# A gated delta rule in two chunks: cross products of the chunks' keys and queries in place of the state, and key products in half-precision pairs

## The chip, the cores and the metric

The kernel runs on one core of one Trainium2 chip. The metric is the device time of one execution in microseconds (us), the median of several runs. The weights and inputs are single precision in DRAM and so is the output.

## The reference, cut to what matters

One block of a network over x of 8 sequences, 256 tokens and 256 channels: adaptive layernorm, a gated delta rule with 16 key heads of 128 and two value heads of 128 for each, a gated output projection, then a feed-forward part that keeps 2 of 4 hidden values. The part that the change touches is this recurrence, for each sequence, head and value head:

```
q = l2norm(conv(x Wq)); k = l2norm(conv(x Wk)); v = conv(x Wv)
S = 0
for t in tokens:
    dv = beta_t * (v_t - k_t S)
    S  = decay_t * S + k_t dv^T
    o_t = q_t S
out = o * rsqrt(mean(o*o) + 1e-6) * norm_w * silu(z)
```

The kernel does not walk the tokens. It cuts a sequence into two chunks of 128 tokens. In a chunk, all dv come from one triangular system whose entries are products of keys with keys, times decays (the matrix A); outputs come from products of keys with queries, times decays (the matrix P). What the first chunk leaves for the second is the state S = K1^T (scaled values of chunk 1), 128 by 256; the second chunk needs K2 S and Q2 S.

## The kernel before, in words

The main part is a loop of 64 steps (16 heads by 4 blocks). A step is one head and one block of two sequences (BG = 2), that is four tiles of 128 tokens (TL = 4) and eight systems of 128 by 128 (U = 8). The steps are software pipelined by hand. Each engine has a function body(s0, s1, s2, s3) (lines 823, 1282, 1763 and 472), called 65 times, which writes out the order in which that engine does the work of four steps at once: s0 is new, s1 is one step older, s2 two, s3 three. Nothing else sets the order; each engine works through its list, and semaphores (sig, need) hold it where a result is missing. Two closing bodies (last_bodies, lines 996, 1354, 1834, 489) finish the last steps beside the beginning of the feed-forward part.

The chain of one step, with its names:

- project (line 597) multiplies hidden rows by the head's weights, both split into two half-precision parts, three products each: keys (0), queries (1), values (2, 3). last_tap (1084, ScalarE) and three convolve (1523, VectorE) for each make the convolution from PSUM into cc.
- turn_keys, turn_queries (633, 639) transpose cc; squares (1113) and squared_norms (1534), guarded_norms (1540), key_norm (382, GpSimd, a power of -0.5 into rn) and keys_normed (1120) give the normed keys kn; turn_normed (645) turns them back and keys_turned (1128) keeps them as knT, in single precision. queries_kept (1134) keeps the second chunk's queries as qT.
- key_key (651) and key_query (657) are four single-precision products each. decayed_keys (1565) and decayed_queries (1575) on VectorE multiply them with decays into at (ae) and pt.
- unit_system, first_inverse and six levels of level_rows, level_left, level_right (677 to 707, with 1160, 1164 and 1600) invert the systems by doubling, then residue (710) and refine (723) correct the inverse once. These all are half-precision products of 64 or 128 columns.
- first_values (733) solves for chunk 1; first_kept (1175) keeps the result twice: u0, and us scaled for the state. **state** (743) multiplies kn of chunk 1 with us, 256 columns, twice; **state_kept** (1187) copies it to st. key_state (757) multiplies knT of chunk 2 with st, query_state (763) qT with st. Then second_rest (1618), second_values (770), second_output (778, 1629), the norm and gate, and project_output (624).

Eight PSUM banks: bP (2) for project, decay_product, z_rows and outputs, bB (2) for the transposes and key products, bS (2) for residue to second_output, bL (2) for the levels. TensorE executes a single-precision product as two MATMUL records each with its own weight load; a transpose or a half-precision product is one.

The order at the head of TensorE's body, which the change rewrites:

```
if s0: bank_project(0, s0, s2); project(0, s0)
if s2: level_right(4, s2); level_left(4, s2)
if s1: key_query(s1)
if s2: level_rows(5, s2)
if s0: bank_project(1, s0, s2); project(1, s0)
```

Of the kernel before, what the change touches and what calls it, by code (L numbers as in the profile page):

```python
# [34 lines left out]
EPS_LN, EPS_RMS, EPS_K2 = 1e-5, 1e-6, 1e-24  # L35
GUARD = 0.25
# [9 lines left out]
def adaln_deltanet_ffn(nc, x, wh, nw, wba, dtb, alog, wgate, wup, wdown, cT, wmod, out):  # L46
    with ExitStack() as ctx:  # L47
# [56 lines left out]
        knT = sb("knT", [P, 2, TL, P])  # L104
        qT = sb("qT", [P, 2, BG, P])
# [16 lines left out]
        us, u0, st, rr, u1, qs = (sol[:, i] for i in range(6))  # L122
# [25 lines left out]
        small = knT[:].rearrange("p r t s -> p (r t s)")  # L148
# [14 lines left out]
        g_abs = qT[0:B].rearrange("p r g s -> p (r g s)").rearrange("p (h c) -> p h c", h=2)  # L163
# [59 lines left out]
        def all_steps(eng, body, last_bodies):  # L223
            for i in range(STEPS + 1):
                body(*lags(i))
            for i in range(STEPS + 1, STEPS + MOST):
                last_bodies(*lags(i)[2:])
# [23 lines left out]
        def _(sp):  # L251
# [38 lines left out]
            sp.wait_ge(sig("qk"), STEPS)  # L290
# [28 lines left out]
        def _(pool):  # L319
# [52 lines left out]
            def decay_operand(s):  # L372
# [4 lines left out]
                for part in range(2):  # L377
                    gp.tensor_tensor(g_le[:, part], le16[:].unsqueeze(1).broadcast_to([P, U, P]),  # L378
                                     hg[:, par(s), part, ts].rearrange("p t v -> p (t v)").unsqueeze(2)
                                     .broadcast_to([P, U, P]), ALU.mult).then_inc(sig("g_le"), 1)  # L380

# [90 lines left out]
            def body(s0, s1, s2, s3):  # L472
                if s3:
                    gate_output(s3)
                if s1:
                    first_inverse(s1)
                if s0:
                    decay_operand(s0)
                if s3:
                    output_scale(s3)  # L480
                    scaled_output(s3)
                if s1:
                    low_half(s1)
                if s0:
                    key_norm(s0)
                    masked_beta(s0)
                    decay_beta(s0)

            def last_bodies(s2, s3):

# [4 lines left out]
                else:  # L495
# [9 lines left out]
                else:  # L505
# [17 lines left out]
        def _(pe):  # L523
# [126 lines left out]

            def key_key(s):
                need(pe, "knT", N(s) + 1)
                for t in range(TL):
                    ins = m(bB[0][:, t * P:t * P + P], knT[:, ring(s), t], knT[:, ring(s), t])
                ins.then_inc(sig("kk_ps"), 1)

            def key_query(s):
                need(pe, "knT", N(s) + 1)
                for t in range(TL):
                    ins = m(bB[1][:, t * P:t * P + P], knT[:, ring(s), t], cc[:, 1, t * P:t * P + P])  # L660
                ins.then_inc(sig("kq_ps"), 1)

# [80 lines left out]
            def state(s):  # L743
                need(pe, "us", N(s) * 4 + 4)
                for g in range(BG):
                    ins = m(bS[1][:, g * C:g * C + C], kn[:, ring(s), 2 * g], us[:, g * C:g * C + C])
                ins.then_inc(sig("s_ps"), 1)

# [8 lines left out]
            def key_state(s):  # L757
                need(pe, "st", N(s) + 1)
                for g in range(BG):
                    ins = m(bS[1][:, g * C:g * C + C], knT[:, ring(s), 2 * g + 1], st[:, g * C:g * C + C])  # L760
                ins.then_inc(sig("ks_ps"), 1)

            def query_state(s):
                need(pe, "o0", N(s) + 1)
                need(pe, "qk", N(s) + 1)
                for g in range(BG):
                    ins = m(bS[0][:, g * C:g * C + C], qT[:, ring(s), g], st[:, g * C:g * C + C])
# [55 lines left out]
            def body(s0, s1, s2, s3):  # L823
# [3 lines left out]
                if s2:  # L827
                    level_right(4, s2)
                    level_left(4, s2)
                if s1:  # L830
                    key_query(s1)
                if s2:
                    level_rows(5, s2)
# [3 lines left out]
                if s2:  # L837
                    level_left(5, s2)
                if s1:
                    need(pe, "at", N(s1) + 1)  # L840
                    turn_values(0, s1)
                if s2:
                    level_right(5, s2)
                if s1:
                    need(pe, "pt", N(s1) + 1)
# [11 lines left out]
                if s0:  # L857
                    bank_project(3, s0, s2)
                    project(3, s0)
                if s2:  # L860
                    first_values(s2)
                if s1:
                    level_rows(0, s1)
                if s0:
                    need(pe, "iv", N(s0) * 2)
                    turn_keys(s0)
                    turn_queries(s0)
                if s3:
                    bank_turn_output(0, s0, s3)
                    turn_output(0, s3)  # L870
                if s2:
                    state(s2)
                if s1:
                    level_left(0, s1)
                if s2:
                    first_output(s2)
                if s1:
                    level_right(0, s1)
                if s2:
                    key_state(s2)  # L880
                if s3:
# [6 lines left out]
                if s0:  # L888
                    bank_decays(0, s0, s3)
                    decay_product(0, s0)  # L890
# [5 lines left out]
                if s0:  # L896
                    bank_decays(1, s0, s3)
                    decay_product(1, s0)
                    turn_normed(s0)
                if s2:  # L900
                    second_output(s2)
# [3 lines left out]
                if s1:  # L905
                    level_rows(2, s1)
                if s3:
                    bank_output(1, s0)
                    project_output(1, s3)
                if s1:  # L910
                    level_left(2, s1)
                    level_right(2, s1)
                if s0:
                    key_key(s0)
                if s1:
                    level_rows(3, s1)
                    bank_z(0, s0, s3)
                    z_rows(0, s1)
                    level_left(3, s1)
# [3 lines left out]
                    level_right(3, s1)  # L923
# [72 lines left out]
            def last_bodies(s2, s3):  # L996
                if s2:
                    level_right(4, s2)
                    level_left(4, s2)
                    level_rows(5, s2)  # L1000
                    level_left(5, s2)
# [4 lines left out]
                else:  # L1006
                    gate(1)
                bank_turn_output(0, None, s3)
                turn_output(0, s3)
                if s2:  # L1010
                    state(s2)
# [3 lines left out]
                    key_state(s2)  # L1015
                bank_turn_output(1, None, s3)
# [918 lines left out]
```

## Time and profile before

| | us |
|---|---|
| median of 3 runs | 2161.03 |
| lowest, highest | 2156.39, 2161.54 |
| the profiled execution's own time | 2155.69 |
| its span, first to last instruction | 2153.9 |
| mean granted TensorE clock | 0.986 of full speed |
| TensorE (PE) busy | 2068.8, 96% |
| VectorE (DVE) busy | 1890.6, 88% |
| ScalarE (ACT) busy | 1599.1, 74% |
| GpSimd (POOL) busy | 1317.9, 61% |

The profiled execution took 2155.69 us, 5.3 below the median of the runs; its span leaves out 1.8 us around it. Matmul ends are modelled and overlap the next matmul's start, so a block's cost on TensorE is read from its start to the start of the next block.

### The profile page before, as it was taken

The numbers are of one execution on the slowest core, as the hardware profiler recorded it, in microseconds if no ns is written. First come the engines' busy times: TensorE is split into PE (matmuls) and PEld (weight loads), VectorE is DVE, ScalarE is ACT, GpSimd is POOL, SyncE is SP. The second block draws the span as 40 slices with busy tenths as digits, with TensorE's granted clock in tenths as the row PEclk, the third lists the DMA queues.
The fourth block names the chain that finished last, engine by engine and source line by source line (L and its number), as shares of the span: only waits on it lengthen the run. The fifth ranks groups of instructions, "written<-read, shape, count | busy, mean of one in ns | idle before, by whom it ended". The sixth has DMA issues, their size and how long they took to land. (4 is left out here: it accounts for less than half of the span.)

```text
span 2153.9 us, 59276 instructions
## 1 busy us (share of the span) xinstructions
PE 2068.8 (96%) x22950; PEld 1709.5 (79%) x22950; DVE 1890.6 (88%) x3119; ACT 1599.1 (74%) x3275; POOL 1317.9 (61%) x832
## 2 busy tenths in 40 slices
PE   5599999999999999999999999999999999997898
PEld 4378888888888888888888888888888888886787
DVE  5689888899888898888898888898888998886898
ACT  3477788887778887878877878877888877776332
POOL 3456666666666666666666666666666666663452
PEclk7899999999999999999999999999999999999999
DMA  2000000000000000000000000000000000002000
GB/s 103 8 4 19 2 21 2 22 2 22 2 22 2 21 2 2 21 2 21 2 22 2 21 2 21 2 2 21 2 22 2 22 2 21 2 2 91 23 23 23
DMA packets 12392, 33.90 MB, mean 16 GB/s; under 512 B 1100, under 2 KB 9420, under 8 KB 9684
## 3 DMA queue, kind: packets, MB, share of 16 engines
q1 hardware_dynamic: 12116, 30.11, 4.0%
q8 instruction: 187, 3.06, 0.6%
q14 instruction: 89, 0.73, 0.1%
HBM read 27.99 MB, written 2.11 MB: 14 GB/s over the span
## 5 line engine op out<-in xcount | busy, mean ns | idle before, releaser
L1531 DVE SCALAR_TENSOR_TENSOR cc<-bank,wc,cc 128x510 f32<-128x510 f32 (+2 forms) x768 | 546.9, 739 | 20.7 <-ACT cc L1096 16.0
L527 PE MATMUL bank<-h,w 128*128 128x512 f16 (+1 forms) x1920 | 419.0, 359 | 9.6 <-DVE cc L1531 3.1
L1606 DVE TENSOR_TENSOR yl<-bank,mask 128x512 f16<-128x512 f32 x384 | 262.7, 684 | 63.9 <-PE bank L527 63.9
L527 PEld LDWEIGHTS bank<-h,w 128*128 128x128 f16 x1920 | 171.5, 98 | 149.6 <-DVE cc L1531 19.6
L1166 ACT ACTIVATE invT<-bank 128x512 f16<-128x512 f32 x384 | 235.6, 614 | 59.2 <-PE bank L527 59.2
L1162 ACT ACTIVATE inv<-bank 128x512 f16<-128x512 f32 x384 | 232.0, 604 | 59.4 <-PE bank L527 59.4
L1096 ACT ACTIVATE cc<-bank,wc 128x512 f32<-128x512 f32 x256 | 177.8, 695 | 129.1 <-PE bank L527 129.1
L378 POOL TENSOR_TENSOR g_le<-le,hg 128x1024 f16<-128x1024 f16 x128 | 239.7, 1893 | 23.4 <-DVE hc L1492 23.4
L404 POOL TENSOR_TENSOR e_b<-ae,b_le 128x1024 f32<-128x1024 f32 x64 | 151.5, 2367 | 158.7 <-ACT ae L1152 158.7
L446 POOL TENSOR_TENSOR invT<-maskT,a 128x1024 f16<-128x1024 f16 x64 | 136.0, 2126 | 161.6 <-DVE a L1589 161.6
L386 POOL TENSOR_TENSOR rn<-n2m,mhalf 128x4 f32<-128x4 f32 x64 | 64.8, 1013 | 276.2 <-DVE n2m L1546 276.2
L527 PE MATMUL bank<-inv,a 128*128 128x64 f16 (+1 forms) x3584 | 218.0, 197 | 3.2 <-ACT inv L1162 2.2
L527 PEld LDWEIGHTS bank<-inv,a 128*128 128x128 f16 x3584 | 188.9, 98 | 17.9 <-ACT inv L1162 2.9
L412 POOL TENSOR_TENSOR osq<-o,zg 128x1024 f32<-128x1024 f32 x64 | 151.4, 2366 | 75.3 <-DVE oss L1643 75.3
L527 PE MATMUL bank<-w,goT 128*128 128x256 f16 x1536 | 188.3, 273 | 2.1 <-DVE goT L1656 2.1
L527 PE MATMUL bank<-w,h 128*128 128x256 f16 x1536 | 189.3, 273 | 0.0
L527 PEld LDWEIGHTS bank<-yl,invT 128*128 128x128 f16 x3072 | 132.8, 98 | 52.0 <-DVE yl L1606 39.4
L527 PE MATMUL bank<-yl,invT 128*128 128x64 f16 x3072 | 153.8, 193 | 10.1 <-DVE yl L1606 10.1
L527 PEld LDWEIGHTS bank<-w,goT 128*128 128x128 f16 x1536 | 146.0, 98 | 17.7 <-DVE goT L1656 2.3
L1228 ACT ACTIVATE zth<-bank 128x512 f32<-128x512 f32 x128 | 76.1, 594 | 108.0 <-PE bank L527 108.0
L527 PE MATMUL bank<-invT,yl 128*128 128x64 f16 x3072 | 153.9, 193 | 1.9 <-DVE yl L1606 1.1
L527 PEld LDWEIGHTS bank<-w,h 128*128 128x128 f16 x1536 | 141.8, 98 | 14.9
(212 smaller groups left out, 5297.1 us busy)
## 6 DMA issues: line engine op xcount, KB each, us to landing
w_raw<-in_wh SPq DMA_DIRECT2D x16, 1032.0 KB, 4.8
v<-in_x SPq DMA_DIRECT2D x4, 512.0 KB, 3.8
out<-sol SPq DMA_DIRECT2D x16, 128.0 KB, 1.7
w_raw<-in_wgate SPq DMA_DIRECT2D x1, 1024.0 KB, 4.7
cc<-in_wup SPq DMA_DIRECT2D x1, 1024.0 KB, 4.7
pt<-gate_store SPq DMA_DIRECT2D x2, 512.0 KB, 4.3
ae<-in_wdown SPq DMA_DIRECT2D x1, 1024.0 KB, 6.7
sol<-gate_store SPq DMA_DIRECT2D x2, 512.0 KB, 5.8
```

The source lines that it names most:

```text
L378: gp.tensor_tensor(g_le[:, part], le16[:].unsqueeze(1).broadcast_to([P, U, P]), hg[:, par(s), part, ts].rearrange("p t v -> p (t v)").unsq ...
L386: gp.tensor_tensor(rn[:], n2m[:, blk(s), 0], mhalf[:, 0:TL], ALU.pow).then_inc(sig("rn"), 1)
L404: gp.tensor_tensor(e_b[:, :, 1:P + 1], e_raw, b_le[:], ALU.mult).then_inc(sig("eb"), 1)
L412: gp.tensor_tensor(flat(osq[:]), o[:].rearrange("p t v d -> p (t v d)"), flat(zg[:]), ALU.mult).then_inc(sig("zo"), 1)
L446: gp.tensor_tensor(invT[:, ring(s)], maskT1[:].unsqueeze(1).broadcast_to([P, U, P]), a1[:, ring(s)], ALU.mult).then_inc(sig("it"), 1)
L527: return mm(o_, l_, r_, start=start, stop=stop, skip_group_check=True)
L1096: A(cc[:, i], bP[i % 2][:], ACT.Copy, scale=wc[:, par(s), i, 3:4]).then_inc(sig("tap"), 1)
L1162: A(lefts(inv[:, ring(s)], l), halves(bL[0], l), ACT.Copy).then_inc(sig("x_ready"), 1)
L1166: A(rights(invT[:, ring(s)], l), halves(bL[1], l), ACT.Copy).then_inc(sig("xt_ready"), 1)
L1228: A(zth[:, 2 * h:2 * h + 2].rearrange("p t d -> p (t d)"), bP[h][:], ACT.Tanh, scale=0.5 / W_SCALE).then_inc(sig("z_tanh"), 1)
L1531: V.scalar_tensor_tensor(dst, src, wc[:, par(s), i, 3 - j:4 - j], dst, ALU.mult, ALU.add).then_inc(sig(f"conv{i}"), 1)
L1606: V.tensor_tensor(lefts(yl[:, l], l), halves(bL[0], l), left(mask[:, l + 1, :], l).unsqueeze(1).broadcast_to([P, U, HP // n_, n_]), ALU.mu ...
```

## The change

The state is gone. By K2 S = (K2 K1^T)(scaled values), the kernel multiplies chunk 1's keys with chunk 2's keys and with chunk 2's queries (key_cross, new), keeps both products (kx) and multiplies those with us. To have such products cheaply, normed keys and queries, scaled by 16, are kept as pairs of half-precision numbers (k16, q16, high and low part); key_key, key_query and key_cross are each three half-precision products in place of one of single precision. state, state_kept and queries_kept are gone, keys_low (VectorE), queries_high (ScalarE), queries_low (GpSimd) and cross_kept (ScalarE) are new, keys_turned writes the high part. The scale is taken out again in the decay columns in the setup. The bodies of all four engines are in a new order.

Products and copies:

```
-            def key_key(s):   m(bB[0][t], knT[t], knT[t])             (x4, f32)
-            def key_query(s): m(bB[1][t], knT[t], cc[1, t])           (x4, f32)
-            def state(s):     m(bS[1][g], kn[2g], us[g])              (x2, f32, 256 columns)
+            def key_pairs(o_, s, t, other, t_other):
+                for i, (a, b_) in enumerate(((0, 0), (0, 1), (1, 0))):
+                    ins = m(o_, k16[:, a, t], other[:, b_, t_other], start=(i == 0), stop=(i == 2))
+            def key_key(s):   need kh, kl; key_pairs(bB[0][t], s, t, k16, t)     (x4)
+            def key_query(s): need kl, ql; key_pairs(bB[1][t], s, t, q16, t)     (x4)
+            def key_cross(s):
+                need(pe, "pt", N(s) + 1)
+                for g in range(BG):
+                    for i, other in enumerate((k16, q16)):
+                        c_ = (g * 2 + i) * P
+                        ins = key_pairs(bB[1][:, c_:c_ + P], s, 2 * g, other, 2 * g + 1)
             def key_state(s):
-                need(pe, "st", N(s) + 1)
+                need(pe, "us", N(s) * 4 + 4)
+                need(pe, "kx", N(s) + 1)
-                    ins = m(bS[1][g], knT[:, ring(s), 2 * g + 1], st[g])
+                    ins = m(bS[1][g], kx[:, ring(s), g, 0], us[g])
             def query_state(s):
-                    ins = m(bS[0][g], qT[:, ring(s), g], st[g])
+                    ins = m(bS[0][g], kx[:, ring(s), g, 1], us[g])
```

The other engines:

```
 ScalarE
-                A(knT[:, ring(s)], grid(bB[1]), ACT.Copy).then_inc(sig("knT"), 1)
+                A(k16[:, 0], grid(bB[1]), ACT.Copy).then_inc(sig("kh"), 1)
-            def queries_kept(s): A(qT, second chunk of cc[:, 1], ACT.Copy)
+            def queries_high(s): A(q16[:, 0], cc[:, 1], ACT.Copy).then_inc(sig("qh"), 1)
+            def cross_kept(s):   need kx_ps; A(kx[:, ring(s)], grid(bB[1]), ACT.Copy).then_inc(sig("kx"), 1)
-            def state_kept(s):   A(st, bS[1][:], ACT.Copy).then_inc(sig("st"), 1)
 GpSimd
+            def queries_low(s):  need qh; gp.tensor_tensor(q16[:, 1], cc[:, 1], q16[:, 0], ALU.subtract)
 VectorE
+            def keys_low(s):     need kh; V.tensor_tensor(k16[:, 1], grid(bB[1]), k16[:, 0], ALU.subtract)
-  one tensor_scalar for the taps of a head
+  three tensor_scalar for the taps of a head (the queries' tap times 16)
+  setup: one tensor_scalar more over cols[:, BETA]
```

TensorE's body, new order in full, in place of lines 823 to 923:

```
project(0,s0) key_query(s1) level_left(4,s2) project(1,s0) level_rows(5,s2) level_right(4,s2)
key_cross(s1) turn_values(0,s1) level_left(5,s2) level_right(5,s2) turn_values(1,s1) residue(s2)
project(2,s0) turn_system(s1) refine(s2) project(3,s0) level_rows(0,s1) first_values(s2)
turn_keys(s0) level_right(0,s1) turn_queries(s0) level_left(0,s1) key_state(s2) first_output(s2)
turn_output(0,s3) turn_output(1,s3) query_state(s2) level_rows(1,s1) second_values(s2)
level_left(1,s1) level_right(1,s1) decay_product(0,s0) second_output(s2) level_rows(2,s1)
decay_product(1,s0) turn_normed(s0) project_output(0,s3) project_output(1,s3) level_left(2,s1)
key_key(s0) level_right(2,s1) level_rows(3,s1) z_rows(0,s1) level_right(3,s1) level_left(3,s1)
z_rows(1,s1) level_rows(4,s1)
```

On VectorE decayed_queries moves from behind level_rows(5) of the next body to the end of its own body, as decayed_queries(s0), so that it stands ahead of the next body's first convolve; keys_low(s0) stands between level_rows(2) and output_sums. On ScalarE cross_kept(s1) stands behind inverse_right(4), queries_high(s0) behind inverse_right(2), and high_half moves from the next body to a place between inverse_left(3) and inverse_right(3). On GpSimd the order becomes gate_output, queries_low, low_half, output_scale, first_inverse, decay_operand, masked_beta, scaled_output, key_norm, decay_beta. turn_values(1) now waits for kx in place of pt.

## Rows read from the trace of the kernel before

**Rows 1.** The page, busy time of each engine, its share, and instructions.
```profile
PE 2068.8 (96%) x22950; PEld 1709.5 (79%) x22950; DVE 1890.6 (88%) x3119; ACT 1599.1 (74%) x3275; POOL 1317.9 (61%) x832
```

**Rows 2.** Busy time by stage (us, instructions), granted clock last, a steady stretch.
```profile
600.00:800.00 200.00, 199.36 (x2325) 164.81 (x2325) 179.43 (x287) 160.24 (x332) 132.61 (x76) 1.00 0.04 12
```

**Rows 3.** ScalarE's queries_kept: once a step; first and last start.
```profile
L1138 ACT ACTIVATE qT<-cc x64: 407/417/421, 86.7 to 1938.6; 128x256 f32<-128x256 f32 x64
```

**Rows 4.** Timeline of TensorE over one step: start, modelled length, operation.
```profile
993.78 1.46 PE L527 MATMUL bank<-h,w 128*128 128x512 f16 x6
...
996.77 1.46 PE L527 MATMUL bank<-h,w 128*128 128x512 f16 x6
998.18 0.41 PE L527 MATMUL bank<-yl,invT 128*128 128x64 f16 x8
...
998.90 0.40 PE L527 MATMUL bank<-invT,yl 128*128 128x64 f16 x8
999.31 0.66 PE L530 MATMUL bank<-ident,cc 128*128 128x128 f32 x4
999.80 0.22 PE L527 MATMUL bank<-inv,a 128*128 128x128 f16 x1
...
1000.64 0.22 PE L527 MATMUL bank<-inv,a_lo 128*128 128x128 f16 x1
1000.70 1.46 PE L527 MATMUL bank<-h,w 128*128 128x512 f16 x6
1001.99 0.61 PE L527 MATMUL bank<-ident,a 128*128 128x128 f16 x8
1002.44 0.61 PE L527 MATMUL bank<-invT,hm 128*128 128x128 f16 x8
1003.12 1.47 PE L527 MATMUL bank<-h,w 128*128 128x512 f16 x6
...
1006.90 1.03 PE L527 MATMUL bank<-sol,kn 128*128 128x256 f32 x4
1007.77 0.41 PE L527 MATMUL bank<-yl,invT 128*128 128x64 f16 x8
...
1018.70 1.14 PE L527 MATMUL bank<-knT 128*128 128x128 f32 x8
...
1023.23 1.46 PE L527 MATMUL bank<-h,w 128*128 128x512 f16 x6
...
1025.01 1.14 PE L527 MATMUL bank<-cc,knT 128*128 128x128 f32 x8
1025.98 0.40 PE L527 MATMUL bank<-inv,a 128*128 128x64 f16 x8
```

**Rows 5.** Groups by shape, TensorE: refine, busy us and mean ns, idle before.
```profile
L527 PE MATMUL bank<-invT,hm 128*128 128x128 f16 x512 | 39.6, 220 | 0.2
```

**Rows 6.** Timeline of VectorE in the same step, two of its rows.
```profile
996.00 1.53 DVE L1531 SCALAR_TENSOR_TENSOR cc<-bank,wc,cc 128x510 f32<-128x510 f32 x2 [0.21 <-ACT cc L1096]
...
1002.33 1.40 DVE L1531 SCALAR_TENSOR_TENSOR cc<-bank,wc,cc 128x506 f32<-128x506 f32 x2
```

**Rows 7.** Groups by shape on ScalarE, VectorE and GpSimd: busy us, mean ns, idle.
```profile
L1191 ACT ACTIVATE sol<-bank 128x512 f32<-128x512 f32 x64 | 41.1, 642 | 0.6 <-PE bank L527 0.6
L1110 ACT ACTIVATE w<-w_raw 128x512 f16<-128x512 f32 x60 | 39.4, 657 | 0.0
L1132 ACT ACTIVATE knT<-bank 128x512 f32<-128x512 f32 x64 | 37.2, 581 | 0.2 <-PE bank L530 0.2
...
L1597 DVE TENSOR_TENSOR inv<-bank,mask 128x512 f16<-128x512 f32 x128 | 81.8, 680 | 0.4 <-PE bank L527 0.4
...
L419 POOL TENSOR_TENSOR a_lo<-ae,a_hi 128x1024 f16<-128x1024 f32 x64 | 136.9, 2139 | 0.6 <-ACT a_hi L1158 0.6
```

**Rows 8.** Who waited for whom: us in total, times, longest.
```profile
POOL rn L386 <- DVE n2m L1546: 276.2, 64, 8.3
...
DVE o L1635 <- PE bank L527: 101.7, 64, 2.3
```

More of the change, by code:

```diff
@@ L475, in body @@
                 if s1:
+                    queries_low(s1)
+                    low_half(s1)
+                if s3:
+                    output_scale(s3)
+                if s1:
                     first_inverse(s1)
@@ L832, in body @@
                 if s2:
-                    level_rows(5, s2)
+                    level_left(4, s2)
                 if s0:
@@ L837, in body @@
                 if s2:
-                    level_left(5, s2)
+                    level_rows(5, s2)
+                    level_right(4, s2)
                 if s1:
+                    key_cross(s1)
                     need(pe, "at", N(s1) + 1)
@@ L866, in body @@
                     turn_keys(s0)
+                if s1:
+                    level_right(0, s1)
+                if s0:
+                    need(pe, "iv", N(s0) * 2)
                     turn_queries(s0)
+                if s1:
+                    level_left(0, s1)
+                if s2:
+                    key_state(s2)
+                    first_output(s2)
                 if s3:
@@ L896, in body @@
                 if s0:
+                    bank_decays(0, s0, s3)
+                    decay_product(0, s0)
+                if s2:
+                    second_output(s2)
+                if s1:
+                    level_rows(2, s1)
+                if s0:
                     bank_decays(1, s0, s3)
@@ L1005, in last_bodies @@
                     first_values(s2)
[L1006 to L1011, printed above, removed]
+                    key_state(s2)
                     first_output(s2)
@@ L1014, in last_bodies @@
                     turn_hidden(1)
-                    key_state(s2)
-                bank_turn_output(1, None, s3)
+                bank_turn_output(0, s0, s3)
+                turn_output(0, s3)
+                bank_turn_output(1, s0, s3)
                 turn_output(1, s3)
@@ L1286, in body @@
                     inverse_left(4, s2)
-                if s1:
-                    queries_kept(s1)
+                if s0:
+                    split_weights(s0)
+                    last_tap(1, s0)
                 if s2:
                     inverse_right(4, s2)
-                if s0:
-                    last_tap(1, s0)
+                if s1:
+                    cross_kept(s1)
                 if s2:
@@ L1311, in body @@
                 if s2:
+                    first_scaled(s2)
+                if s0:
+                    squares(0, s0)
+                if s2:
                     first_kept(s2)
@@ L1314, in body @@
                     squares(1, s0)
-                if s3:
-                    output_high(0, s3)
-                if s2:
-                    state_kept(s2)
-                if s0:
-                    squares(0, s0)
-                if s2:
-                    first_output(s2)
                 if s1:
@@ L1325, in body @@
                     inverse_right(0, s1)
+                if s2:
+                    first_output(s2)
                 if s3:
+                    output_high(0, s3)
                     output_high(1, s3)
@@ L1803, in body @@
                 if s3:
+                    output_low(0, s3)
                     output_low(1, s3)
+                if s2:
+                    second_output(s2)
                 if s0:
                     split_weights(s0)
-                if s2:
-                    if s1 and not s0:
+                if s1:
+                    if not s0:
                         gate_weights_low(2)
                         gate_weights_low(3)
-                    second_output(s2)
-                if s1:
                     level_rows(2, s1)
+                if s0:
+                    keys_low(s0)
                 if s2:
@@ L1832, in body, with last_bodies @@
                             gated(j)
-            def last_bodies(s2, s3):
+                if s0:
+                    decayed_queries(s0)
+            def last_bodies(s0, s1, s2, s3):
+                if not s2:
+                    silu(0)
+                    hidden_stats(TL)
+                    hidden_product(0)
                 if s2:
+                    level_rows(5, s2)
+                    correction(s2)
                     for j in range(TL):
                         hidden_stats(j)
-                    level_rows(5, s2)
-                    correction(s2)
                     for j in range(TL):
```

232 lines of the change are left out of this document (114 added, 118 removed).

## The prediction

> **What bounds the kernel now.** I read the busy shares first [rows 1]: TensorE 96%, VectorE 88%, ScalarE 74%, GpSimd 61%. Busy TensorE is not proof of a TensorE bound, so next the stages: in a steady stretch of 200 us it is busy 199.36 at the full clock of 2.4 GHz, VectorE 179.43, ScalarE 160.24, GpSimd 132.61 [rows 2]. Then the length of a step: ScalarE's once-a-step copy starts first at 86.7 and last at 1938.6, 63 steps of 29.40 us [rows 3], and project(0) starts at 993.78 and again at 1023.23, 29.45 later [rows 4]. So 1852 of 2153.9 us are this loop, and the rest is setup and feed-forward, which the change hardly touches.
>
> Since matmul ends are modelled, short stalls do not show as idle. The timeline does show them, if one takes the spacing of blocks. Products of 128 columns come every 0.056 us (16 from 999.80 to 1000.70; the 8 from 1001.99 to 1002.44), so refine, from 1002.44, was done at 2.89, and project(3) started at 3.12: 0.23 of stall. project takes 1.29 (1000.70 to 1001.99), so project(1) at 996.77 was done at 8.06 and its follower came at 8.18: 0.12. The level products from 998.90 are worth 0.24 (that is what they take wherever nothing waits) and the next block came 0.41 later: 0.17 [rows 4]. With a few hundredths more that is about 0.57 us between project(0) and project(3), which are 9.34 apart. From project(3) to the next project(0) I find none: 20.11 us of blocks at their unhindered spacing. TensorE therefore has 28.86 us of work a step and 0.6 of stall, and the stall has one cause: project(3) must have VectorE's last convolution of the queries, the first of the pair that starts at 1002.33 and takes half of 1.40, so ends at 3.03 [rows 6]. VectorE was in unbroken work from 996.00 to there. So the first third of a step is a VectorE path, the other two thirds are pure TensorE.
>
> **The change on TensorE.** Removed per step: key_query 0.97 (1025.01 to 1025.98), key_key the same by its equal modelled 1.14, state 0.87 (1006.90 to 1007.77), in sum 2.81. Added: three groups of 12 half-precision products of 128 columns, 36 in all. Price by the nearest rows, which are the same shape with a weight load of their own each and, in residue, the same accumulation in one PSUM region: 0.90/16 = 0.0563 us, so 2.03 [rows 4]. Net 0.78 us less: 28.08 of work. The upper bound for the price is what the groups view books for refine, 39.6 us busy over 512, 0.077 each [rows 5]; that counts the modelled tail of each block, and the spacings speak for 0.056. At the upper bound it is 36 x 0.077 = 2.78, and the saving is gone.
>
> The Trainium skill, TensorE: Matmul & The Clock Gate, section "Back-to-back issue gap", speaks against this change: in a stream of pairs of weight load and matmul it gives about 81 ns per product of 128 columns, against an isolated gap of 56. By it, 36 products are an estimated 2.92 us, more than the 2.81 removed, and the kernel would be 0.11 us a step slower. Here the trace disagrees: the stream of 16 such pairs runs at 56 ns.
>
> **Where it lies in the step.** Between project(0) and project(3) TensorE gains key_cross (+0.68) and loses 0.29 in key_query: work 8.77 - 0.29 + 0.68 = 9.16. VectorE does the same ten operations there as before, only with decayed_queries first. It used to begin at 2.22 behind project(0) (996.00, held 0.21 by ScalarE's tap) [rows 6]; now it must wait for key_query, which ends at 1.29 + 0.68 and with the same latency as the tap is seen at about 2.2. So project(3) starts about 9.3 to 9.4 in both kernels: here nothing is won, and the added key_cross is paid from the stall that was there. The rest has 28.08 - 9.16 = 18.92 of work. If it stays without stall, a step is 9.34 + 18.92 = 28.26. But its latencies get tighter; what is late next, by walking the new order with durations of the rows: key_state now comes 0.4 behind the point where ScalarE has scaled us, query_state waits for first_output's copy, which stands behind squares and two inverse copies (about 0.25 late), turn_output(1) for the last convolution (0.1), second_output for u1 and qs (0.1). I take 0.3 for these after overlaps, bounds 0 and 0.8. **Step: 28.56, against 29.45, 0.89 less.**
>
> **VectorE.** Added: keys_low, like first_inverse's half in shape: 81.8/128 = 0.64 [rows 7], and two small scalings a head. Load 179.43/200 x 29.45 = 26.4, new 27.1 of 28.56, 95%. Its waits must fit in 1.46, where they were 3.0. The largest, second_output's for TensorE, 101.7/64 = 1.6 [rows 8], becomes shorter because VectorE now comes later to it. keys_low waits for the high part; it stands behind level_rows(2), and by then ScalarE should be done. Behind it wait output_sums, then the adds and decayed_keys; output_squares is late by the new copies, and GpSimd's gate follows.
>
> **ScalarE.** Gone: state_kept 0.64, keys_turned 0.58, queries_kept 0.42; new: high part of keys 0.58 and cross_kept 0.58 by the PSUM copy, queries_high 0.66 by the split of weights [rows 3, 7]. +0.2 on 23.6: 23.8 of 28.56, hidden, unless one is in the way: cross_kept stands before inverse_left(5), which residue wants, worth 0.1 at most.
>
> **GpSimd.** queries_low is half of low_half's 2.14, so 1.07 (bounds 1.07 and 2.14) [rows 7]; load 19.5 + 1.1 = 20.6. It runs after gate_output, well before key_query. key_norm used to wait 276.2/64 = 4.3 us a step [rows 8]; masked_beta (and scaled_output) moved ahead of it use that gap. If they ran over, rn, kn and turn_normed would be late; by the walk they end 3 us before.
>
> **Waits added.** turn_values(1) waits for kx rather than pt; key_cross for pt. decayed_queries is done at about 3.35 behind project(0), TensorE reaches key_cross at 3.98, so 0.6 to spare; cross_kept is done at 5.4 and is wanted at 5.6. Both can cost a tenth or two.
>
> **Ends.** Setup: one more VectorE operation over 512 columns and small ones, up to +0.7 with its wait. Tail: once, product 0.87 and copy 0.64 less in a chain that has no cover: -1.5. Net -1. DMA issues do not move in number.
>
> **Sum.** Some 61 steps are in the steady regime (the first and the last pair wait on chains): 61 x 0.89 = 54, and the ends 1: 2155.7 - 55 = 2100.7 for an execution like the profiled one. The median of the runs stands 5.3 above it: **2106 us**.
>
> **Rivals.**
> (a) *The stalls go altogether*, the work of 28.08 sets the pace: 1.37 x 61 = 84, 2077. Against it: VectorE path to project(3). Chance 0.07.
> (b) *Latency eats most of the gain*: key_cross and kx, query_state and second_output together cost 0.8 to 1.2 rather than 0.3, a step of 29.1 to 29.2, TensorE visibly waiting on ScalarE: gain 15 to 22, about 2141. For it: four chains now meet at 95% of VectorE. Chance 0.14.
> (c) *Half-precision products of 128 columns cost as much as what they replace*, 0.077 or more: 2.78 against 2.81, no change, 2159; the change would then not do what it is made of. Against it: the spacing in rows 4. With the price of the page named above it would be 2168. Chance 0.04, half of it within 0.3%, half slower.
> (d) *VectorE becomes the bound*, the side of slower: work 27.1 plus waits. From 2.35 us of waits a step on, nothing is won; were they to stay at 3.0 because decayed_queries, put ahead of the first convolve, holds seven convolutions behind key_query, the step is 30.1, 0.7 longer, 61 x 0.7 = 43: 2204. For it: in-order VectorE with a new wait at its head and one at keys_low. Against it: key_query comes directly behind project(0), for whose tap VectorE waited anyhow. Chance 0.03.
> The forecast holds the remaining 0.72.
>
> Differences of 0.3%, 6.5 us, are what a measurement of this kernel can tell. **Chances:** faster 0.92 (forecast, (a) and nearly all of (b)), within 0.03 (half of (c), the edge of (b)), slower 0.05 ((d), half of (c)). **Range:** the forecast with its bounds 0 and 0.8 of stall reaches from 2087 (1.19 x 61 + 1 less) to 2136 (0.39 x 61 + 1 less); I take 2080 to 2138, which holds the forecast and part of (a) and of (b).
>
> **What would show it.** Right: steps 28.3 to 28.8 apart; the three groups of 12 at 0.68 each; project(3) 9.3 to 9.4 behind project(0); VectorE at 94 to 95% in the steady stretch and its wait before second_output under 1 us; TensorE still over 99% busy there. Wrong: spacing of the pairs near 0.08 (c); VectorE waiting on key_query by over 0.5 us, or project(3) starting over 9.8 (d); TensorE idle before key_cross, query_state or second_output by more than 0.5 in sum (b).

## The result and the profile after

The changed kernel takes 2142.4 us (median of 4 runs, 2141.9 to 2142.5) against 2158.71 us of the kernel before (4 runs). The ratio is 0.9924, 95% interval 0.9907 to 0.9941: faster by 0.8%, about 16 us, where 55 were forecast. The time lies 4 us above the top of the range.

The busy times of the page, as in [rows 1]:

```profile
PE 2038.0 (95%) x23974; PEld 1686.3 (79%) x23974; DVE 1954.9 (91%) x3216; ACT 1632.9 (76%) x3275; POOL 1404.1 (66%) x896
```

TensorE is busy 31 us less, but the time fell by half of that, and TensorE's share with it. The stage view says the same, against [rows 2]: 197.0 of 200 us busy, where it was 199.4.

```profile
600.00:800.00 200.00, 197.00 (x2439) 163.28 (x2438) 189.71 (x303) 165.64 (x332) 142.84 (x83) 1.00 0.04 13
```

A mean over 200 us hides where 2.4 us of TensorE idle lie. decayed_queries runs once a step on VectorE; in the kernel before its 64 starts are 29.45 us apart, all but the first two distances and the last. In the changed kernel, with the same three left out, they are 28.64 apart three times and 30.65 the fourth, 15 times over. Here are one long and one short step side by side (stage view: us, busy PE, PEld, DVE, ACT, POOL):

```profile
959.73:990.37 30.64, 29.14 (x362) 23.91 (x359) 29.29 (x48) 24.28 (x50) 20.52 (x13) 1.00 0.10 36
990.37:1019.01 28.64, 28.64 (x362) 23.88 (x359) 26.89 (x43) 24.28 (x50) 20.63 (x13) 1.00 0.01 2
```

TensorE issues the same 362 products in both. VectorE has five instructions more in the long one and 2.4 us more busy time, and 2.4 us is far too much for five small ones (three scalings of the taps and two copies). VectorE's timeline of the long step:

```profile
977.99 0.69 DVE L1675 TENSOR_TENSOR o<-bank,sol 128x512 f32<-128x512 f32 x1 [0.93 <-PE bank L539]
978.60 0.68 DVE L1592 SCALAR_TENSOR_TENSOR w<-w_raw,w 128x512 f16<-128x512 f32 x1
979.20 0.16 DVE L1548 TENSOR_SCALAR wc<-w_raw 128x4 f32<-128x4 f32 x1
979.27 0.17 DVE L1549 TENSOR_SCALAR wc<-w_raw 128x4 f32<-128x4 f32 x1
979.34 0.17 DVE L1550 TENSOR_SCALAR wc<-w_raw 128x8 f32<-128x8 f32 x1
979.41 2.36 DVE L1521 COPY hg<-g_cols 128x64 f16<-128x64 f16 x1
981.69 0.21 DVE L1522 COPY hc<-cols 128x128 f32<-128x128 f32 x1
981.82 0.68 DVE L1646 TENSOR_TENSOR yl<-bank,mask 128x512 f16<-128x512 f32 x1
```

and GpSimd's and TensorE's at the same time:

```profile
979.33 2.39 POOL L415 TENSOR_TENSOR e_b<-ae,b_le 128x1024 f32<-128x1024 f32 x1 [3.37 <-ACT ae L1183]
```

```profile
982.56 0.41 PE L539 MATMUL bank<-yl,invT 128*128 128x64 f16 x8 [0.88 <-DVE yl L1646]
983.25 0.83 PE L539 MATMUL bank<-k 128*128 128x128 f16 x12 [0.28 <-DVE k L1603]
...
984.88 1.48 PE L539 MATMUL bank<-w,h 128*128 128x256 f16 x12 [0.34 <-DVE y_acc L1707]
```

A copy of 64 half-precision columns, the next head's decays, takes 2.36 us. It starts 0.08 us after GpSimd's decay_beta and ends at 981.77, 0.05 behind its end. Level 2's rows, the low half of the keys and the adds come late behind it on VectorE, and TensorE waits for each: 0.88, 0.28 and 0.34, in sum the 1.5 us that it is idle in the long step. The copies ahead of the change, then after it (the view of one line; durations are least, median and largest in ns):

```profile
L1491 DVE COPY hg<-g_cols x16: 174/181/186, 65.2 to 1809.0; 128x64 f16<-128x64 f16 x16
```

```profile
L1521 DVE COPY hg<-g_cols x16: 189/2355/2358, 66.2 to 1795.3; 128x64 f16<-128x64 f16 x16
L1522 DVE COPY hc<-cols x16: 213/215/222, 66.3 to 1797.6; 128x128 f32<-128x128 f32 x16
```

The change moved VectorE's weight split, with these column copies behind it every fourth step, from ahead of second_output to behind it. The account of the change ahead of the prediction does not name this move; it is one of the many in the new order. It took the copies from a moment when GpSimd is idle, as the kernel before shows, into decay_beta:

```profile
984.47 0.18 DVE L1491 COPY hg<-g_cols 128x64 f16<-128x64 f16 x1
984.57 0.22 DVE L1492 COPY hc<-cols 128x128 f32<-128x128 f32 x1
```

```profile
986.43 2.37 POOL L404 TENSOR_TENSOR e_b<-ae,b_le 128x1024 f32<-128x1024 f32 x1 [2.54 <-ACT ae L1152]
```

15 long steps at 2.0 us more are 30 us.

The rest of the account, spans against spans: 2153.9 - 2140.7 = 13.2 us. decayed_queries starts first at 90.13 (88.24 before), 1.9 later; from the first to the last start are 1830.4 us (1851.7 before), 21.3 won; from there to the end are 220.2 (214.0 before), 6.2 lost. How much of the two losses belongs to the change is taken up below.

### The profile page after: what moved, and what is told of

Same layout as the page of the kernel before. It is cut to its first block and busy times, and to the rows that moved or that the text cites. A ratio compares the mean times of both kernels' runs of the same rounds, so it can differ in the third digit from the quotient of the medians.

```text
span 2140.7 us, 61867 instructions
## 1 busy us (share of the span) xinstructions
PE 2038.0 (95%) x23974; PEld 1686.3 (79%) x23974; DVE 1954.9 (91%) x3216; ACT 1632.9 (76%) x3275; POOL 1404.1 (66%) x896
## 5 line engine op out<-in xcount | busy, mean ns | idle before, releaser
L1567 DVE SCALAR_TENSOR_TENSOR cc<-bank,wc,cc 128x510 f32<-128x510 f32 (+2 forms) x768 | 535.0, 738 | 3.2 <-ACT cc L1118 3.0
L415 POOL TENSOR_TENSOR e_b<-ae,b_le 128x1024 f32<-128x1024 f32 x64 | 151.8, 2372 | 214.0 <-ACT ae L1183 214.0
L430 POOL TENSOR_TENSOR a_lo<-ae,a_hi 128x1024 f16<-128x1024 f32 x64 | 151.2, 2363 | 54.9 <-ACT a_hi L1189 54.9
L539 PE MATMUL bank<-w,goT 128*128 128x256 f16 x1536 | 179.8, 274 | 2.1 <-DVE goT L1696 2.1
L539 PEld LDWEIGHTS bank<-w,goT 128*128 128x128 f16 x1536 | 150.9, 98 | 19.6 <-DVE goT L1696 2.3
L542 PE MATMUL bank<-ident,cc 128*128 128x128 f32 x1024 | 158.3, 277 | 0.2 <-ACT kx L1170 0.2
```

What stands on the lines that cost most here:

```text
L415: gp.tensor_tensor(e_b[:, :, 1:P + 1], e_raw, b_le[:], ALU.mult).then_inc(sig("eb"), 1)
L430: gp.tensor_tensor(a_lo[:, ring(s)], at, a_hi[:], ALU.subtract).then_inc(sig("al"), 1)
L539: return mm(o_, l_, r_, start=start, stop=stop, skip_group_check=True)
L542: return nc.tensor.transpose(o_, i_, id_)
L1567: V.scalar_tensor_tensor(dst, src, wc[:, par(s), i, 3 - j:4 - j], dst, ALU.mult, ALU.add).then_inc(sig(f"conv{i}"), 1)
```

## The experiments

e1, e2 and e4 are the changed kernel with one edit, e3 is the kernel before with one. e5 to e10 are built on e1: they hold its move as well as the edit shown. Their times stand beside runs of the kernel before on the same chip; e2, e3 and e6 to e9 have one run each.

### e1: the weight split ahead of second_output

```
-                if s2:
-                    second_output(s2)
                 if s0:
                     split_weights(s0)
+                if s2:
+                    second_output(s2)
```

> The changed kernel with one move on VectorE: the weight split, with the next head's tap scalings and column copies, stands ahead of second_output again, as in the kernel before. In the changed kernel three steps of four take 28.64 us and every fourth, the one with the column copies, 30.65; there the copy of 128x64 half-precision columns took 2.36 us where it took 0.18 before, and it began within 0.1 us of GpSimd's decay_beta, which lasted 2.39. Theory P (the copy is held for as long as GpSimd's instruction runs): at the new place GpSimd is idle, the copy takes 0.2, every fourth step falls to 28.7 or less, and 15 x 2.0 = 30 us go: about 2112. Besides, the split fills the wait of 0.93 ahead of second_output, so all steps may lose up to 0.3: down to 2095. Rival R (the fourth step is long because VectorE has more operations in it, 0.8 us, or because it holds back the next head's weights): place doesn't matter much, fourth step stays at 30 or more, 2135 to 2142.

2111.48 us (2106.7 to 2111.7), ratio 0.977, interval 0.9755 to 0.9784. Every step is 28.64 us, the fourth ones too; the copy takes 0.18:

```profile
L1521 DVE COPY hg<-g_cols x16: 177/182/189, 66.7 to 1768.7; 128x64 f16<-128x64 f16 x16
```

```profile
600.00:800.00 200.00, 200.00 (x2487) 166.69 (x2485) 189.11 (x311) 169.59 (x343) 143.07 (x85) 1.00 0.04 13
```

So the 30 us are the place of the copies, and the rival (more operations, or the next head's weights late) falls: the same instructions are still in the fourth step. The other three steps kept 28.64, so filling the wait of 0.93 ahead of second_output was worth nothing to them, where I had allowed up to 0.3.

That the medians lie 30.9 us apart as well is in part chance. In the spans (31.0) the long steps give the 30; the first two distances between the starts of decayed_queries cost 3.8 (TensorE was granted 0.90 of its full speed from 89.49 to 160 us, 0.97 in the changed kernel from 90.13), and setup and closing part are 4.6 shorter.

### e2: the single-precision copy first

```
-                V.tensor_copy(hg[:, p_], g_cols[:, :, :, hs]).then_inc(sig("hc"), 1)
                 V.tensor_copy(hc[:, p_], cols[:, :, :, hs]).then_inc(sig("hc"), 1)
+                V.tensor_copy(hg[:, p_], g_cols[:, :, :, hs]).then_inc(sig("hc"), 1)
```

> The changed kernel with the two column copies of a head in the other order: the single-precision one (128x128) first, the half-precision one (128x64) second. It tells whether the hold belongs to the type or to the moment. Theory P (any plain copy from SBUF to SBUF is held while GpSimd works): the single-precision copy now takes about 2.3 us and the half-precision one 0.2, time unchanged at 2142. Rival (only the half-precision copy is held, or the copy has a cost of its own in the data it reads): the single-precision copy stays at 0.2, and the half-precision copy takes about 2.2; the time is the same too, so the rows decide.

```profile
L1522 DVE COPY hg<-g_cols x16: 172/174/184, 66.1 to 1795.4; 128x64 f16<-128x64 f16 x16
...
L1521 DVE COPY hc<-cols x16: 228/2395/2402, 65.9 to 1793.1; 128x128 f32<-128x128 f32 x16
```

Whichever copy comes first is held, in either type, and the other is free. The long steps are 30.64 as before. The one run took 2135.5 us; of the 7 us to the changed kernel 0.4 are in the loop, 1.8 ahead of it (decayed_queries starts first at 88.29, against 90.13) and 4.6 in the closing part (215.6 from the last decayed_queries, against 220.2).

### e3: the kernel before, with its copies moved into decay_beta

```
             split_weights(s): if q == 3:
-                    head_columns(head(s) + 1, to)
 body:               second_output(s2)
+                if s0:
+                    next_columns(s0)      # head_columns of the next head if blk(s0) == 3
                 if s1:
                     level_rows(2, s1)
```

> The kernel before, with the two column copies moved from ahead of second_output to directly behind it, where GpSimd has been in decay_beta (2.37 us) for 0.3 us. Theory P: the half-precision copy takes about 2.0 us there, level_rows(2) is about 1.3 us late once in four steps, and TensorE, which is the bound, passes on 1 to 1.3 of it: 15 to 20 us slower, 2172 to 2180, with every fourth step at 30.5 or so. Rival R (the hold needs something of the changed kernel): the copy stays at 0.2 us and the time at 2156 to 2161.

2172.79 us, 13.3 above the median of the kernel before on the same chip (2159.05 to 2162.12). VectorE and GpSimd around one copy:

```profile
991.88 0.69 DVE L1638 TENSOR_TENSOR o<-bank,sol 128x512 f32<-128x512 f32 x1 [1.57 <-PE bank L527]
992.49 2.09 DVE L1491 COPY hg<-g_cols 128x64 f16<-128x64 f16 x1
994.50 0.21 DVE L1492 COPY hc<-cols 128x128 f32<-128x128 f32 x1
```

```profile
992.17 2.37 POOL L404 TENSOR_TENSOR e_b<-ae,b_le 128x1024 f32<-128x1024 f32 x1 [2.53 <-ACT ae L1152]
```

The copy came 0.32 us into GpSimd's instruction (0.08 in the changed kernel), lasted 0.27 less, and ended at 994.58, again 0.04 behind GpSimd's 994.54. That is the mark of a hold to the end of the other instruction, not of a slow one. Every fourth step is 30.33 in place of 29.45, 0.9 more, so 15 x 0.9 = 13 us. I had expected 1 to 1.3 a long step: less of the delay reached the next step than I thought.

### e4: the same columns by a reduction

```
-                V.tensor_copy(hg[:, p_], g_cols[:, :, :, hs])
+                V.tensor_reduce(hg[:, p_] as (a t) v, g_cols as (a t) h [:, :, hs].unsqueeze(3), AXX, ALU.max)
```

> The changed kernel, everything in its place, but the half-precision columns are written by a reduction over an axis of length one in place of the copy: the same elements at the same moment, by another kind of instruction. The Trainium skill, SBUF - State Buffer, has copies among the operations that can take the port pair shared with GpSimd and says that a reduction never does. Theory P in this form: the instruction takes 0.2 to 0.3 us beside GpSimd's decay_beta; then the single-precision copy behind it either is held in its place (about 2.1 us, time stays at 2142) or is not (2112). Rival R (what is held is the access to these columns, whatever reads them): the reduction takes 2.3 us, 2142.

```profile
L1521 DVE TENSOR_REDUCE hg<-g_cols x16: 209/212/220, 67.1 to 1795.7; 128x64 f16<-128x64 f16 x16
...
L1524 DVE COPY hc<-cols x16: 216/2266/2271, 67.2 to 1795.8; 128x128 f32<-128x128 f32 x16
```

The reduction passed beside GpSimd in 0.21 us, and the copy behind it was held in its place, 2.27 us. 2137.08 us, ratio 0.9893 (0.9876 to 0.9909), long steps 30.54 to 30.56; the 5 us to the changed kernel lie ahead of the loop (1.7) and in the closing part (5.0), not in the loop, which is 2.0 longer. So neither the half-precision data nor the place in memory is held, but the plain copy. A kernel with both columns written by reductions was not run.

The Trainium skill, SBUF — State Buffer, section "Who interferes with whom", has this: copies can enter a mode that takes the port pair shared with GpSimd, whoever starts first keeps it for a whole instruction, and a reduction does not contend. The changed kernel, e2, e3 and e4 agree, with 2.36, 2.40, 2.09 and 2.27 us for held copies and 0.21 for the reduction. The Trainium skill's account by ports is its own; these runs show who is held and until when.

### e5: first_output's copy ahead of two inverse copies

```
                 if s2:
+                    first_output(s2)
                 if s1:
                     inverse_left(0, s1)
                     inverse_right(0, s1)
-                if s2:
-                    first_output(s2)
```

> On top of e1 (weight split and column copies early), one move on ScalarE: first_output's copy goes ahead of inverse_left(0) and inverse_right(0). In e1 a step is 28.64 us where the TensorE work by its unhindered spacing is 28.08; of the difference, query_state starts with the end of that copy (962.67 against 962.71), the eight transposes ahead of it take 0.95 in place of 0.88, and query_state 0.97 in place of 0.87. Theory S (the remainder is short waits that also expose the first weight load behind them): the copy is done 0.95 earlier, query_state begins up to 0.08 earlier and takes 0.87, so 0.1 to 0.18 less a step, 61 times: 6 to 11 us, 2100 to 2105. Rival W (single-precision groups simply take 0.97 behind others): no change, 2111.

2136.93 us, ratio 0.989 (0.9873 to 0.9906): 25 us slower than e1, all steps 29.03. A miss. Theory S was right about query_state, which now takes 0.87, and wrong about the rest. ScalarE and what TensorE waits for:

```profile
971.04 0.60 ACT L1227 ACTIVATE o<-bank 128x512 f32<-128x512 f32 x1 [0.76 <-PE bank L539]
971.53 0.59 ACT L1193 ACTIVATE inv<-bank 128x512 f16<-128x512 f32 x1
972.01 0.60 ACT L1197 ACTIVATE invT<-bank 128x512 f16<-128x512 f32 x1
```

```profile
PEld bank L539 <- ACT sol L1244: 46.6, 64, 2.2
```

ScalarE waits 0.76 us for TensorE at the copy's new place, with two inverse copies behind it that could have filled the time. second_kept (line 1244) then comes late, and the weight load of second_output waits 46.6/64 = 0.73 a step for it (0.05 in e1). second_output starts 0.83 behind decay_product(0), and 0.44 in e1 (936.89 to 937.33): these 0.39 are what the step grew by.

```profile
974.51 0.60 PE L539 MATMUL bank<-g_le,gt 128*128 128x512 f16 x2
975.34 1.16 PE L539 MATMUL bank<-sol,pt 128*128 128x128 f32 x8 [0.22 <-ACT sol L1244]
```

### e6: keys_low twice

```
+                V.tensor_tensor(k16[:, 1], grid(bB[1]), k16[:, 0], ALU.subtract).then_inc(sig("kl_first"), 1)
+                need(dve, "kl_first", N(s) + 1)
                 V.tensor_tensor(k16[:, 1], grid(bB[1]), k16[:, 0], ALU.subtract).then_inc(sig("kl"), 1)
```

> On top of e1, VectorE does keys_low twice (same result), with a wait between: 0.65 to 0.7 us a step more on VectorE, which then is busy about 97% of a step, and the low half of the keys 0.7 later. VectorE waits about 1.1 to 1.9 us a step in e1. Theory T (TensorE sets the pace, VectorE has slack behind keys_low, where output_sums waits 0.25 and key_query's product 0.25): 0 to 0.3 us a step, 2111 to 2130. Rival D of the prediction (VectorE is the bound already): 0.65 a step, 2150.

2117.59 us, steps 28.73 to 28.74. 0.64 us more work on VectorE cost 0.1. VectorE, at 95% busy in e1 (189.11 of 200), is near its limit but does not set the pace.

### e7 and e8: low parts left out of key_cross, and of key_key

```
 e7, in key_cross:
-                        ins = key_pairs(bB[1][:, c_:c_ + P], s, 2 * g, other, 2 * g + 1)
+                        ins = m(bB[1][:, c_:c_ + P], k16[:, 0, 2 * g], other[:, 0, 2 * g + 1])
 e8, in key_key:
-                    ins = key_pairs(bB[0][:, t * P:t * P + P], s, t, k16, t)
+                    ins = m(bB[0][:, t * P:t * P + P], k16[:, 0, t], k16[:, 0, t])
```

> On top of e1, key_cross does only the product of the two high halves: 4 half-precision products of 128 columns in place of 12, so the low parts of the cross products are left out; 8 x 0.056 = 0.45 us less on TensorE a step, all of it between project(0) and project(3). The prediction says that this stretch, 9.25 us in e1, is a path of VectorE (tap, decayed_queries, convolutions, correction, last convolution of the queries): then project(3) stays 9.2 behind project(0) and the time at 2108 to 2112. Rival (TensorE is the bound there too): 0.45 x 61 = 27 us less, 2084.

> On top of e1, the same cut in key_key: 4 products in place of 12, the low parts of the keys' products with keys are left out; 0.45 us less on TensorE a step, this time in the later stretch, between project(3) and the next project(0), which the prediction calls pure TensorE. Expected: all of it, 61 x 0.45 = 27 us, 2084. Rival (the later stretch hangs on VectorE's or ScalarE's chain as well): less than half of it, above 2097.

e7: 2108.14 us, steps 28.57, project(3) 9.19 behind project(0) (952.89 - 943.70) where it was 9.25. As said. e8: 2105.53 us, steps 28.59: 0.45 us of TensorE work gone, 0.05 won. A miss. Its timeline:

```profile
938.97 0.39 PE L539 MATMUL bank<-k 128*128 128x128 f16 x4
939.20 0.40 PE L539 MATMUL bank<-invT,yl 128*128 128x64 f16 x8
939.82 0.41 PE L539 MATMUL bank<-inv,a 128*128 128x64 f16 x8 [0.23 <-ACT inv L1196]
```

The 8 products of level_right(2) from 939.20 are worth 0.24, and level_rows(3) starts 0.62 later: 0.38 of wait for ScalarE's copy of inverse_left(2). key_key stands between that product and its user and covers the latency. I had called everything behind project(3) pure TensorE because I saw no stall there; no stall only means that each latency was covered, and here by the very products that I counted as a price.

### e9: the low half of the gated output left out of project_output

```
-   split_product(...)                       # (0,0) (0,1) (1,0) for both p_: 24 products of 256 columns
+   for n_, (p_, b_) in enumerate(((0, 0), (0, 1), (1, 0), (1, 1))):
+       ins = m(..., goT16[:, 0, t * PV + p_], weights(s, b_, ...))        # 16
```

> On top of e1, project_output leaves out the products with the low half of the gated output: 16 half-precision products of 256 columns in place of 24 a step, 0.87 us less on TensorE. In e1 these products stand where no level product waits for its forerunner: level_left(2) behind them starts 2.2 us after VectorE has written its operand. e7 and e8 took 0.45 from places that cover the latency of the level chain and gained 0.06 each. Theory C (a cut pays where it uncovers no latency, up to the next limit): most of 0.87 is won at first, until VectorE, which waits 1.1 to 1.9 us a step, is held by nothing: 0.4 to 0.87 a step, 2058 to 2087. Rival L (all engines now hang in one ring of latencies, and no cut on TensorE pays): under 0.15 a step, 2103 to 2111.

2096.46 us, steps 28.44: 0.20 won of 0.87, between the two theories. The reason is again ScalarE's order:

```profile
931.88 0.39 PE L539 MATMUL bank<-yl,invT 128*128 128x64 f16 x8 [0.52 <-ACT invT L1197]
```

level_left(2) waits for inverse_right(1), which stands behind the copies of the keys and output_squares. The 16 products from 929.45 are worth 1.75 (0.109 each), and level_left(2) starts 2.43 behind their start: 0.68 of the 0.87 went into this wait. What would limit the kernel without it, no run here tried.

### e10: level_rows(1) ahead of query_state

```
+                if s1:
+                    level_rows(1, s1)
                 if s2:
                     query_state(s2)
-                if s1:
-                    level_rows(1, s1)
-                if s2:
                     second_values(s2)
```

> On top of e1, level_rows(1) goes ahead of query_state on TensorE, so that 0.24 us of other work lies between the transposes and query_state, which in e1 starts the moment ScalarE's copy of first_output is done. Nothing is moved on the in-order engines. Theory S: query_state starts 0.2 later than in e1 or less, finds its operand there, takes 0.87 in place of 0.97, and the transposes ahead run at 0.88: 0.1 to 0.18 us less a step, 2100 to 2106. Rival (ScalarE's query_part and second_kept behind it come as much later as in the run with the copy moved, and second_output waits): slower than e1 by 0.1 to 0.4 a step, 2117 to 2135.

2106.15 us (5 runs, 2102.3 to 2108.1), ratio 0.9746, interval 0.9733 to 0.9759; steps 28.56, 0.08 less than e1. The intervals of e10 and of e1 (0.9755 to 0.9784) overlap a little; the steps of their profiles, the same 60 times over, are clear. Theory S had the place right and the price wrong: query_state takes 0.95 there and not 0.87, though ScalarE's copy for it was done 0.30 us before. This is the fastest kernel that computes everything, 54 us below the kernel before on its chip and by the medians 36 below the changed one.

## Why the prediction was wrong

**The reading of the kernel before and the bound** held. Steps of 29.45 with about 0.6 of stall, TensorE in front, and project(3) held by the last convolution of the queries: in the changed kernel project(3) starts 9.25 behind project(0), 988.21 to 997.46 (forecast 9.3 to 9.4), and in e7 0.45 us less TensorE work in this stretch moved it by 0.06.

**The price of the products** held. The changed kernel's timeline, with key_key, key_query and the first of key_cross's four groups of three, and what follows each of them:

```profile
1012.39 0.83 PE L539 MATMUL bank<-k 128*128 128x128 f16 x12
1013.06 0.40 PE L539 MATMUL bank<-invT,yl 128*128 128x64 f16 x8
...
1018.14 0.83 PE L539 MATMUL bank<-q,k 128*128 128x128 f16 x12
1018.81 0.40 PE L539 MATMUL bank<-yl,invT 128*128 128x64 f16 x8
...
1020.81 0.33 PE L539 MATMUL bank<-k 128*128 128x128 f16 x3
...
1021.48 0.61 PE L542 MATMUL bank<-ident,cc 128*128 128x128 f32 x4
```

Twelve products take 0.67 each time: 0.056 a product. Rival (c) fell. The Trainium skill, TensorE: Matmul & The Clock Gate, section "Back-to-back issue gap", gives about 81 ns for such a pair of weight load and matmul; this trace, with 56 ns, disagrees.

**The step** was 28.56 by forecast and is 28.64 in three steps of four. The 0.3 us that I took for stalls and lost cover behind project(3) measured 0.47 (19.39 against 18.92 of work). Some 60 steps at 0.08: 5 us, a term mis-sized within its bounds.

**The step of the argument that failed** is the part on VectorE: "Added: keys_low ... and two small scalings a head." It priced what was added and not what was moved, and so put the moved column copies at nothing. They go past second_output with the weight split, and at the new place they meet GpSimd's decay_beta: 2.36 us for the first of them in place of 0.18, and 2.0 us more for each of 15 steps. The copies cost 0.4 us together in the kernel before, where GpSimd was idle, and I neither gave their row nor asked. e1 (take the move back: every fourth step falls from 30.65 to 28.64), e3 (move the copies alone in the kernel before: 13.3 us slower) and e2 and e4 (which instruction is held) show it. The same place was a cheap choice in the old kernel for one reason more: there VectorE waited at second_output anyhow.

**The ends** were put at 1 us of gain and lost 8: 1.9 ahead of the loop and 6.2 behind the last decayed_queries. I had allowed 0.7 for the setup. Most of this is not the change. e1, e2 and e4 to e10 have the changed kernel's setup and start decayed_queries first at 87.8 to 89.8; e3 has the old setup and starts it at 87.87. Behind the last decayed_queries the time goes with the granted clock of the first 110 us there, though not in strict order (e6 has 0.86 and 217.1 us):

| | granted clock | us to the end |
|---|---|---|
| kernel before | 0.95 | 214.0 |
| e3 (old closing part) | 0.89 | 218.4 |
| e4 | 0.95 | 215.2 |
| e2 | 0.94 | 215.5 |
| changed kernel | 0.92 | 220.2 |
| e5 | 0.89 | 220.0 |

By the pairs at a like clock (0.95 and 0.89) the new closing part is 1 to 2 us longer than the old one. The 1.5 us that the prediction took off for state and state_kept do not show. What decides the clock there was not tried.

**Together,** in the spans: 30 for the held copies, 9 for the ends and 5 for the steps make 44; the first and last distances between steps and the count of steps give back 2, and 42 is what lies between forecast (55) and measured gain (13.2). The medians are 16 apart because the profiled execution of the kernel before, with 2155.69 us, was shorter than its four runs (median 2158.71).

**The rivals.** (a) did not come. (b) gave 2141, which is nearly the time measured, but not its mechanism: its 29.1 to 29.2 in every step is not what the trace shows. Its sum is wrong too: 0.8 to 1.2 on 28.26 are 29.06 to 29.46, a gain of 0 to 24 us and not of 15 to 22. (d) fell: VectorE waits 0.25 us for key_query and was no bound, as e6 shows; but on its side a single instruction of the 48 in a long step did what I had looked for in its load. With e1's place for the copies, the forecast's 2106 stands against 2111.5. That e10 measures 2106 as well is chance, since it has another order than the one forecast.

**What stays open.** e8 and e9 show that the kernel at 28.6 is held by TensorE and, 0.05 to 0.2 us behind it, by latencies of the level chain through ScalarE. How much of the 0.78 us of saved products could be had by another order is not known.

## What to carry to other kernels

When an edit moves instructions, look at every one of them, the small ones too, and at what the other engines do at the new place: in these runs every plain copy of VectorE from SBUF to SBUF that started inside GpSimd's decay_beta lasted until that instruction ended. A step length taken from the mean of a stage hides a pattern with a period; list the starts of one instruction that comes once a step. And a group of products can be both work and cover: before counting its removal as a gain, see which result is under way meanwhile.

## What the runs showed of the hardware that was not expected

- A VectorE copy from SBUF to SBUF is held until GpSimd's running instruction (decay_beta, the only one met) ends: 0.04 to 0.05 us beyond for the half-precision copy, 0.08 to 0.09 for the single-precision one. 0.18 or 0.22 us become 2.09 to 2.40. A reduction of the same 64 columns at the same moment took 0.21.
- VectorE's operations with one input in PSUM, and its reductions, keep their usual length beside GpSimd. In every short step of the changed kernel keys_low and output_sums start inside decay_beta and take 0.68 and 1.22 us; in the long step above, outside it, they take 0.68 and 1.20. Copies from PSUM are not held either: four of 128x512 that started inside GpSimd's gate_output took 0.68, like the others.

```profile
1010.44 0.68 DVE L1603 TENSOR_TENSOR k<-bank,k 128x512 f16<-128x512 f32 x1
1011.37 1.22 DVE L1683 TENSOR_REDUCE oss<-osq 128x8 f32<-128x1024 f32 x1 [0.24 <-ACT osq L1252]
```

```profile
1009.98 2.37 POOL L415 TENSOR_TENSOR e_b<-ae,b_le 128x1024 f32<-128x1024 f32 x1 [3.38 <-ACT ae L1183]
```

- GpSimd's low_half grew from 2.14 to 2.34 us in the median, unchanged in itself. In its new place it starts while VectorE's unit_system, which reads two operands from SBUF, still runs, and it grows with the time that the two share: 2.13 at 0.09 us, 2.34 at 0.34, 2.37 at 0.37, 2.46 at 0.46. From 0.34 on it has grown by the shared time less 0.14. The other way round, unit_system, 1.22 by itself, takes 1.24 where it starts 0.16 before the end of GpSimd's queries_low and 1.29 where it starts 0.21 before it. So whichever starts second looks held until the first is done. No run here moved one of them to test it.
- Groups of single-precision products take different times for the same columns: query_state 0.96 to 0.97 us in e1, where its operand arrives as it starts, 0.87 in e5, where it was there 0.16 before, but 0.95 in e10, where it was there 0.30 before. What decides this is open.
